# A convolution–attention block: output weights fetched with x on two DMA queues, zero fills earlier and partly on VectorE, PReLU as the larger of two linear forms, norms behind the match convolution

## The chip, the cores and the metric

The kernel runs on one core of a Trainium2 chip. The metric is the device time of one execution in microseconds (us); three timed runs before the change are shown, and one profiled execution of the same kernel.

## The reference, cut to what matters

Two images of 32 channels, 48 x 48, are normalised per channel. A cross-scale attention follows: a match image (1x1 convolution W1, 16 channels, full resolution), a reference image (W2, 16 channels, after 2x2 means) and an embedding (Wa, 32 channels). Each goes through a PReLU.

```
def prelu(x, a):
    return jnp.where(x >= 0, x, a * x)
embed_w  = prelu(conv1x1(x, Wa, ba), aa)
match_in = prelu(conv1x1(x, W1, b1), a1)
ref = prelu(conv1x1(x.mean over 2x2 blocks, W2, b2), a2)
w   = 3x3 patches of ref, each divided by its norm      # 576 keys
xp  = 3x3 patches of match_in                           # 2304 queries
yi  = softmax(10 * w . xp over the keys)
yt  = transposed convolution of yi with 6x6 patches of embed_w, stride 2
yd  = convolution of yt with Wd (3x3, stride 2) + bd, divided by 6
x   = x + yd
x   = x + DCT along h and w of the normalised x
```

## The kernel before

**Work in chunks.** The queries of an image are cut into six chunks of 8 rows x 48 columns (384 queries), each chunk into three tiles of 128 queries: 36 steps for both images. A step computes scores of one tile against 576 keys on TensorE (L707, four pairs of high and low fp32r parts), the row maximum on VectorE (L1156), the exponential on ScalarE (L899), the sum's reciprocal on VectorE (L1163) and the scaling on ScalarE (L907). GpSimd adds neighbouring rows of the softmax tiles (row sums, L528), TensorE turns the sums (L727, transposes by an identity, nine or eighteen to a group), ScalarE and VectorE split them (L915, L1171), and TensorE multiplies them by the embedded values (L742) and by the output weights (L754), which a chunk lags three chunks' steps behind. VectorE adds the result to x (L1194).

**The order.** Every engine has its own queue and runs it strictly in the order written. The list `BEFORE` holds what precedes the first step (image 0: statistics `xs`, `mean`, the split of x `low`, `weights`, `bias`, `conv2` in two parts, `conv1` in eight parts, `squares`, `norm`, `inorm`, `keys`, `split` of the first two chunks). `SPREAD` puts the jobs of image 1, and the embedding of image 0, into numbered gaps of the steps, three gaps to a step; each engine does its own share of a job when it comes to that gap. `split` of chunk g needs the im2col rows of chunk g in SBUF: ScalarE makes the high part, GpSimd the low part (L518, L522), and only then can TensorE compute that chunk's scores.

**A convolution part.** TensorE writes one of two PSUM banks (`pm`, L621 for `conv1` and `conv2`, L660 for the embedding; three matmuls for a `conv1` part). ScalarE writes the positive part `z` (L851), and in every second part the negative part `zneg` as well (L849); in the others VectorE makes it (L1072). VectorE then writes slope * zneg + z to the image (L1078). For the match image, rows that two overlapping blocks share are written a second time by further instructions of 48 columns (L1075, 14 for an image). A bank is free for the part after next when VectorE is done.

**DMA queues.** SyncE's queue issues, in this order: x of image 0 in four pieces (L363), the reference patches of image 0 (six transfers), the match patches of image 0 (36 transfers, L373 and L377), x for the residual (L411), x of image 1, the nine blocks of the output weights `wdf` (L405), the cosine matrix, x of image 1 for the residual, and then the patches of image 1. The small parameters `par` come on ScalarE's queue.

**GpSimd.** It fills the zeros (`zeros()`, L460 to L467) between `mean` and `squares`, and calls `output_weights()` after everything of `BEFORE`, ahead of its first row sum. That function begins with a wait for the nine `wdf` transfers.

```
            first = before.index(("low", 0, 0))
            perform(before[:first], handlers)
            zeros()
            pool.wait_ge(s_tiles, NTILE_EDGES)
            perform(before[first:], handlers)
            output_weights()
            for s in range(steps):
```

## Time and profile before

| | us |
|---|---|
| median of 3 timed runs | 326.76 (324.23 to 326.82) |
| profiled execution, whole | 326.36 |
| its span on the core | 324.6 |
| TensorE matmuls busy in the span | 259.4 |
| TensorE weight loads busy (beside the matmuls) | 240.2 |
| VectorE busy | 173.8 |
| ScalarE busy | 133.1 |
| GpSimd busy | 98.6 |

The profiled execution's own time stands 1.8 us above its span, for what lies around it. Busy shares are means over stages that have different limits, so the stretches have to be read one by one. The granted clock is given as a fraction of TensorE's full speed: 1.00 is 2.4 GHz and 0.50 is 1.2 GHz.

### The profile page before, as it was taken

How to read it: one execution, taken by the hardware profiler on the slowest of the kernel's cores; microseconds unless marked ns; L12 is line 12 of the kernel's file. 1: busy time of each engine (PE TensorE's matmuls, PEld its weight loads, DVE VectorE, ACT ScalarE, POOL GpSimd, SP SyncE). 2: the span in 40 equal slices, each digit the busy share in tenths (PEclk: the TensorE clock that was granted, in tenths of full speed). 3: DMA queues.
4: the chain of work that ended last, by engine and by line, in shares of the span. 5: the costliest groups of instructions: out<-in, count | busy, mean ns of one | idle time of the engine just before them, and what ended most of it. 6: DMA issues, size and time to landing. Idle time of an engine off the chain costs nothing.

```text
span 324.6 us, 4740 instructions
## 1 busy us (share of the span) xinstructions
PE 259.4 (80%) x1698; PEld 240.2 (74%) x1698; DVE 173.8 (54%) x368; ACT 133.1 (41%) x269; POOL 98.6 (30%) x101
## 2 busy tenths in 40 slices
PE   0459529936396979997998999999998899998075
PEld 0448428926375859996998989999987799997074
DVE  3864623254746673377225745555696854543822
ACT  2060236254346452445335674547645442122020
POOL 2710122038546220523514051517845600000000
PEclk9999999577657575599759999999999999999655
DMA  3030034420003000134300000000120000000241
GB/s 73 0 48 3 9 67 72 104 70 2 1 0 50 2 1 0 14 61 72 56 3 0 2 0 3 0 2 0 38 37 2 0 3 0 2 0 2 44 65 36
DMA packets 11495, 7.67 MB, mean 24 GB/s; under 512 B 8497, under 2 KB 10609, under 8 KB 11345
## 3 DMA queue, kind: packets, MB, share of 16 engines
q1 hardware_dynamic: 11264, 7.09, 12.2%
q10 hardware_dynamic: 208, 0.30, 0.3%
q8 instruction: 13, 0.21, 0.3%
q14 instruction: 10, 0.07, 0.1%
HBM read 2.14 MB, written 1.18 MB: 10 GB/s over the span
## 4 chain that ended last, share of the span: by engine, by line
PE 51%; DVE 20%; issue 9%; SPq 9%; ACT 6%; POOL 2%; DMA 2%; DVEq 0%; ACTq 0%; POOLq 0%
PE zt L727 20%; PE yt L742 8%; PE ps L707 5%; PE pm L681 4%; SPq L377 3%; SPq L373 3%; PE pm L621 3%; DVE negm L1156 3%; PE pm L774 3%; PE pm L660 2%; DVE mimg L1078 2%; DVE yl L1171 2%; DVE bnst L988 2%; PE pd L754 2%; DVE mimg L1075 2%
## 5 line engine op out<-in xcount | busy, mean ns | idle before, releaser
L727 PE MATMUL zt<-ident,nt 128*125 128x128 f32 (+1 forms) x720 | 98.0, 290 | 0.0
L727 PEld LDWEIGHTS zt<-ident,nt 128*125 128x125 f32 (+1 forms) x720 | 94.0, 191 | 1.4 <-issue 0.3
L528 POOL TENSOR_TENSOR nt<-nt 128x599 f32<-128x599 f32 (+1 forms) x42 | 56.4, 1342 | 47.9 <-ACT nt L907 40.8
L1171 DVE TENSOR_TENSOR yl<-zt,yh 125x384 fp32r<-125x384 f32 (+1 forms) x60 | 33.4, 557 | 43.9 <-ACT yh L915 15.2
L915 ACT ACTIVATE yh<-zt 125x384 fp32r<-125x384 f32 (+1 forms) x60 | 29.2, 486 | 44.1 <-PE zt L727 44.1
L899 ACT ACTIVATE nt<-ps,negm 128x576 f32<-128x576 f32 x32 | 23.7, 742 | 56.5 <-DVE negm L1156 56.5
L707 PE MATMUL ps<-wh,mh 128*128 128x288 f32 x64 | 18.3, 372 | 17.0 <-POOL mr L522 12.3
L907 ACT ACTIVATE nt<-nt,rps 128x599 f32<-128x599 f32 x36 | 28.6, 795 | 7.1 <-DVE rps L1163 6.9
L1156 DVE TENSOR_REDUCE negm<-ps 128x1 f32<-128x576 f32 x32 | 24.1, 753 | 13.1 <-PE ps L707 13.0
L742 PE MATMUL yt<-yh,kh 125*128 125x384 f32 (+1 forms) x60 | 25.6, 427 | 4.6 <-DVE yl L1171 4.5
L1194 DVE SCALAR_TENSOR_TENSOR v<-pd,v 32x384 f32<-32x384 f32 (+3 forms) x48 | 26.3, 547 | 2.4 <-PE pd L754 0.9
L518 POOL TENSOR_TENSOR ml<-vim,mh 128x384 fp32r<-128x384 f32 x12 | 12.1, 1005 | 49.4 <-ACT mh L871 49.2
L707 PEld LDWEIGHTS ps<-wh,mh 128*128 128x128 f32 x64 | 11.6, 222 | 19.5 <-POOL mr L522 12.7
L742 PE MATMUL yt<-yh,kl 125*128 125x384 f32 (+1 forms) x60 | 21.5, 359 | 0.0
L742 PE MATMUL yt<-yl,kh 125*128 125x384 f32 (+1 forms) x60 | 21.3, 356 | 0.0
L851 ACT ACTIVATE z<-pm,bias 96x288 f32<-96x288 f32 (+1 forms) x24 | 11.7, 491 | 16.2 <-PE pm L621 12.1
L484 POOL TENSOR_TENSOR mv<-mv,mhalf 32x1 f32<-32x1 f32 x2 | 1.1, 544 | 56.4 <-DVE mv L993 56.4
L742 PEld LDWEIGHTS yt<-yh,kh 125*128 125x128 f32 (+1 forms) x60 | 12.1, 201 | 7.5 <-DVE yl L1171 6.7
L621 PE MATMUL pm<-x4h,wsh 32*96 32x288 f32 x16 | 7.8, 496 | 10.3 <-DVE mimg L1078 9.1
L1163 DVE RECIPROCAL rps<-psm 128x1 f32<-128x1 f32 x36 | 5.9, 164 | 18.5 <-ACT nt L899 18.2
L707 PE MATMUL ps<-wl,mh 128*128 128x288 f32 x64 | 15.3, 324 | 0.0
L707 PE MATMUL ps<-wh,ml 128*128 128x288 f32 x64 | 15.2, 322 | 0.0
(165 smaller groups left out, 462.1 us busy)
## 6 DMA issues: line engine op xcount, KB each, us to landing
vim<-mimg SPq DMA_DIRECT2D x24, 72.0 KB, 2.5
v<-mimg SPq DMA_DIRECT2D x36, 24.0 KB, 1.9
x<-x SPq DMA_DIRECT2D x8, 72.0 KB, 2.9
vim<-mimg SPq DMA_DIRECT2D x12, 48.0 KB, 2.2
v<-x SPq DMA_DIRECT2D x2, 288.0 KB, 3.6
x_copy<-v SPq DMA_DIRECT2D x2, 288.0 KB, 2.9
xr<-x_copy SPq DMA_DIRECT2D x4, 144.0 KB, 3.1
out<-res SPq DMA_DIRECT2D x8, 72.0 KB, 2.4
```

The lines of the kernel that those rows point to most:

```text
L528: pool.tensor_tensor(nt[:, dst, (to + 1) * KP + 1:(to + 1) * KP + 1 + n], nt[:, one, (row1 + 1) * KP + 1:(row1 + 1) * KP + 1 + n], nt[:, o ...
L621: last = nc.tensor.matmul(o, w[rows, at:at + width], v, start=n == 0, stop=n == 2)
L681: last = nc.tensor.matmul(o[0:96, n:n + 1], sq[:, at:at + 96], ones[0:96, 0:1], start=r == 0, stop=r == 2)
L707: last = nc.tensor.matmul(scores_of(t)[:, i, 0:HALF], m[:, k, cols], w[b][:, HALF * i:HALF * (i + 1)], start=n == 0, stop=n == 3)
L727: last = nc.tensor.matmul(turned(zt[:, m % 2, :], n, dh, col, JW), keys_at(tile, r + dr, n, shift), ident[:, :], start=at == 0, stop=at == ...
L742: last = nc.tensor.matmul(yt[:, 0:CHUNK], e[b][0:n, blk, :], y[0:n, blk, :], start=blk == 0 and at == 0, stop=blk == KB - 1 and at == 2)
L899: nc.scalar.activation(strided(nt[:, tile_of(g, jb), :], KP + 1, (KP * HL // 2, 2), (KP, HL // 2), (1, WL)), strided(scores_of(t)[:, 0, :] ...
L907: nc.scalar.activation(tile, tile, ACT.Copy, scale=rps[:, k:k + 1]).then_inc(s_pn, 1)
L915: nc.scalar.activation(yh[0:n, blk, :].rearrange("p (h j) -> p h j", j=W), turned(zt[:, m % 2, :], n), ACT.Copy).then_inc(s_yh, 1)
L1156: nc.vector.tensor_reduce(negm[:, t % 2:t % 2 + 1], scores_of(t)[:, :, 0:HALF], AX.XY, ALU.max, negate=True).then_inc(s_mx, 1)
L1171: nc.vector.tensor_tensor(yl[0:n, blk, :].rearrange("p (h j) -> p h j", j=W), turned(zt[:, m % 2, :], n), F(yh[0:n, blk, :]).rearrange("p ...
L1194: nc.vector.scalar_tensor_tensor(out=image, in0=tap, scalar=1.0 / 6.0, in1=image, op0=ALU.mult, op1=ALU.add).then_inc(s_fin, 1)
```

## The change

1. **Loads.** Two of the four pieces of image 0's x go out on ScalarE's queue, ahead of `par`; SyncE issues the other two, then the nine `wdf` blocks, image 1's x, both residual copies of x and the cosine matrix, all ahead of the first patches.
2. **Zeros.** GpSimd does its zero fills first of all (`wdf` and the edges of `nt`). The fills of `emb`, `mr` and `wr` go to VectorE, at the end of `constants()`, ahead of the statistics. `output_weights()` on GpSimd stands ahead of `squares`.
3. **PReLU.** ScalarE writes slope * (y + bias) to `slanted`, and VectorE writes the larger of (y + bias) and `slanted` straight from PSUM: one instruction on each engine for every part. Where a slope is above 1 the larger form is the wrong one, so weights and biases are multiplied by a sign taken from the slope (`slope_signs()`, which waits for `par`), and the sign is undone in `kscale` and `wdf`. The doubled rows of the match image are no longer written part by part; two copies of 336 columns follow the last part.
4. **Order.** `bias` becomes three jobs, one for each convolution. The split of the big x (`low`) goes behind `conv2`; `norm` goes behind all eight parts of `conv1`. The weights of W2 come first on VectorE, then W1, then Wa. For image 1 the jobs `weights`, `bias`, `low`, `squares`, `norm`, `inorm` and `keys` sit in other gaps.

```
 BEFORE = [
-    ("xs", (0,)), ("mean", (0,)), ("low", (0,)), ("weights", (0,)), ("bias", (0,)), ("conv2", (0, 1)),
-    ("conv1", (0, 1)), ("squares", (0,)), ("conv1", (2, 3, 4)), ("norm", (0,)), ("conv1", (5, 6, 7)),
-    ("inorm", (0, 1)), ("keys", (0,)), ("split", (0, 1))]
+    ("xs", (0,)), ("mean", (0,)), ("weights", (0,)), ("bias", (0, 1)), ("conv2", (0, 1)), ("low", (0,)),
+    ("conv1", (0, 1)), ("squares", (0,)), ("conv1", (2, 3, 4, 5, 6, 7)), ("norm", (0,)),
+    ("inorm", (0, 1)), ("keys", (0,)), ("split", (0, 1)), ("bias", (2,))]
...
-    ("emb", 0, 2, 4, 2), ("ek", 0, 2, 9, 2), ("xs", 1, 1, 13, 1), ("mean", 1, 1, 15, 1), ("low", 1, 1, 17, 1),
-    ("weights", 1, 1, 20, 1), ("bias", 1, 1, 23, 1), ("residual", 0, 1, 28, 1), ("conv2", 1, 2, 26, 1),
-    ("conv1", 1, 8, 29, 1), ("squares", 1, 1, 33, 1), ("norm", 1, 1, 35, 1), ("inorm", 1, 2, 38, 1),
-    ("keys", 1, 1, 41, 1), ("emb", 1, 2, 46, 2), ("ek", 1, 2, 51, 2), ("residual", 1, 1, 60, 1),
+    ("emb", 0, 2, 4, 2), ("ek", 0, 2, 9, 2), ("xs", 1, 1, 13, 1), ("mean", 1, 1, 15, 1), ("weights", 1, 1, 19, 1),
+    ("bias", 1, 3, 22, 1), ("residual", 0, 1, 28, 1), ("conv2", 1, 2, 26, 1), ("low", 1, 1, 27, 1),
+    ("conv1", 1, 8, 29, 1), ("squares", 1, 1, 31, 1), ("norm", 1, 1, 37, 1), ("inorm", 1, 2, 40, 1),
+    ("keys", 1, 1, 42, 1), ("emb", 1, 2, 46, 2), ("ek", 1, 2, 51, 2), ("residual", 1, 1, 60, 1),
...
-            load_x(0)
+            load_x(0, range(2))
+            output_weights()
+            load_x(1, range(4))
+            for b in range(B):
+                sp.dma_start(x1(b), x[b].rearrange("c h w -> c (h w)")).then_inc(s_xin[b], 16)
+            sp.dma_start(cosm[:, :], dct).then_inc(s_cos, 16)
             ref_patches(0)
             match_patches(0)
-            sp.dma_start(x1(0), x[0].rearrange("c h w -> c (h w)")).then_inc(s_xin[0], 16)
-            load_x(1)
-            output_weights()
-            sp.dma_start(cosm[:, :], dct).then_inc(s_cos, 16)
-            sp.dma_start(x1(1), x[1].rearrange("c h w -> c (h w)")).then_inc(s_xin[1], 16)
...
             def output_weights():
 
                 pool.wait_ge(s_wdin, 1 + 16 * 9)
+                pool.wait_ge(s_sign, 1)
+                link(pool.tensor_tensor(wdf[:, :], wdf[:, :], sign[:, 2:3].to_broadcast([128, 128]), ALU.mult))
...
-            first = before.index(("low", 0, 0))
+            first = before.index(("squares", 0, 0))
+            zeros()
+            pool.wait_ge(s_tiles, NPOOL_EDGES)
             perform(before[:first], handlers)
-            zeros()
-            pool.wait_ge(s_tiles, NTILE_EDGES)
+            output_weights()
+            pool.wait_ge(s_wd, 1)
             perform(before[first:], handlers)
-            output_weights()
...
-                if k % 2:
-                    nc.scalar.activation(zneg[0:rows, 1, :], o[0:rows, 0:HALF], ACT.Relu,
-                                         bias=nbias[0:rows, which:which + 1], scale=-1.0)
-                nc.scalar.activation(z[0:rows, k % 2, :], o[0:rows, 0:HALF], ACT.Relu,
-                                     bias=bias[0:rows, which:which + 1]).then_inc(s_z, 1)
+                nc.scalar.activation(slanted[0:rows, k % 2, :], o[0:rows, 0:HALF], ACT.Identity,
+                                     bias=sbias[0:rows, which:which + 1],
+                                     scale=par[0:rows, P_A1 + which:P_A1 + which + 1]).then_inc(s_slant, 1)
...
+                nc.vector.memset(emb[:, :], 0.0).then_inc(s_zero, 1)
+                nc.vector.memset(F(mr[:, :, :]), 0.0).then_inc(s_zero, 1)
+                for b in range(B):
+                    nc.vector.memset(F(wr[b][:, :]), 0.0).then_inc(s_zero, 1)
+                dve.wait_ge(s_zero, 4)
...
+            def slope_signs():
+
+                dve.wait_ge(s_par, 48)
+                link(nc.vector.tensor_scalar(sign[:, :], par[:, P_A1:P_A1 + 3], 1.0, -2.0, ALU.is_gt, ALU.mult))
+                nc.vector.tensor_scalar_add(sign[:, :], sign[:, :], 1.0).then_inc(s_sign, 1)
+                dve.wait_ge(s_sign, 1)
+                link(nc.vector.scalar_tensor_tensor(out=kscale[:, :], in0=sign[:, 0:1], scalar=SOFTMAX_SCALE,
+                                                    in1=sign[:, 1:2], op0=ALU.mult, op1=ALU.mult))
...
+                dve.wait_ge(s_slant, k + 1)
+                w = list(dst.shape)[-1]
+                nc.vector.scalar_tensor_tensor(out=dst, in0=o[0:rows, 0:HALF].rearrange("p (h w) -> p h w", w=w),
+                                               scalar=bias[0:rows, which:which + 1],
+                                               in1=slanted[0:rows, k % 2, :].rearrange("p (h w) -> p h w", w=w),
+                                               op0=ALU.add, op1=ALU.max).then_inc(s_free["dve"], 1)
...
+                    nc.vector.tensor_copy(mimg[:, 1 + W:1 + CHUNK],
+                                          mimg[:, 1 + CHUNK * NCH:1 + CHUNK * NCH + n]).then_inc(s_dup[b], 1)
+                    nc.vector.tensor_copy(mimg[:, 1 + last:1 + last + n],
+                                          mimg[:, 1 + CHUNK + W:1 + 2 * CHUNK]).then_inc(s_dup[b], 1)
```

## Rows read from the trace of the kernel before

**Rows 1.** Stretches: start:end, length, busy (instructions) of PE, PEld, DVE, ACT, POOL; clock; DMA

```profile
0.00:46.40 46.40, 21.14 (x98) 17.88 (x98) 25.88 (x71) 12.61 (x24) 13.08 (x27) 1.00 0.18 33
46.40:70.90 24.50, 20.31 (x101) 18.71 (x101) 7.51 (x16) 12.09 (x25) 2.76 (x5) 0.77 0.41 79
70.90:96.40 25.50, 15.39 (x67) 13.62 (x67) 14.30 (x34) 10.26 (x22) 15.63 (x16) 0.63 0.02 7
96.40:123.00 26.60, 21.46 (x94) 18.15 (x93) 17.84 (x36) 15.19 (x30) 9.82 (x8) 0.63 0.10 16
123.00:145.00 22.00, 22.00 (x127) 21.39 (x128) 9.64 (x25) 8.02 (x18) 7.01 (x6) 0.66 0.14 25
145.00:170.00 25.00, 22.98 (x131) 21.26 (x130) 11.48 (x22) 9.37 (x21) 8.75 (x8) 0.80 0.26 45
170.00:299.00 129.00, 123.93 (x997) 119.04 (x995) 76.46 (x147) 62.31 (x128) 41.04 (x35) 1.00 0.03 6
```

**Rows 2.** Timeline up to the first reference convolution: start, length, engine and line, idle before

```profile
2.28 0.24 DVE L1029 MEMSET wsf<- 128x224 f32 x1
...
5.58 0.96 DVE L998 BATCH_NORM_STATS2 bnst<-x 128x6 f32<-128x288 f32 x2 [2.34 <-DMA x<-x]
...
8.45 0.68 POOL L484 TENSOR_TENSOR gm<-gm,mhalf 128x1 f32<-128x1 f32 x1 [1.67 <-DVE gm L1011]
...
9.59 1.04 DVE L1035 TENSOR_SCALAR nslope<-par 128x3 f32<-128x3 f32 x1
...
14.99 0.41 PE L621 MATMUL pm<-x2h,wsh 32*96 32x144 f32 x1
```

**Rows 3.** DMA issues by line: count, KB each, median us from issue to landing

```profile
par<-params ACTq DMA_DIRECT2D x1, 0.6 KB, 3.6
```

**Rows 4.** Timeline from the first convolution to the first scores

```profile
16.57 0.50 ACT L851 ACTIVATE z<-pm,bias 96x288 f32<-96x288 f32 x1 [9.43 <-PE pm L621]
...
18.41 0.52 PE L621 MATMUL pm<-x4h,wsh 32*96 32x288 f32 x1 [1.02 <-DVE wimg L1078]
...
26.17 5.89 PE L681 MATMUL pm<-ones,sq 96*96 96x1 f32 x36 [0.22 <-DVE mimg L1078]
...
37.00 2.85 PE L690 MATMUL pm<-ident,nrm 96*128 96x96 f32 x12 [0.76 <-DVE mimg L1078]
...
38.63 1.86 SPq L373 DMA_DIRECT2D vim<-mimg  x3
...
46.45 0.85 PE L707 MATMUL ps<-wh,mh 128*128 128x288 f32 x2 [6.61 <-POOL mr L522]
```

**Rows 5.** Instructions of lines 1078, 1072 and 1171: count, duration ns min/median/max, first and last start

```profile
L1078 DVE SCALAR_TENSOR_TENSOR mimg<-zneg,par,z x8: 515/516/1741, 20.9 to 124.4; 96x288 f32<-96x288 f32 x8
...
L1072 DVE TENSOR_SCALAR zneg<-pm,bias x12: 503/513/518, 17.2 to 156.5; 96x288 f32<-96x288 f32 x10, 128x288 f32<-128x288 f32 x2
...
L1171 DVE TENSOR_TENSOR yl<-zt,yh x60: 537/558/560, 100.4 to 298.4; 125x384 fp32r<-125x384 f32 x48, 100x384 fp32r<-100x384 f32 x12
```

**Rows 6.** Timeline, TensorE's two longest waits after the first scores

```profile
72.97 0.85 PE L707 MATMUL ps<-wh,mh 128*128 128x288 f32 x2 [5.67 <-POOL mr L522]
...
85.98 0.39 PEld L602 LDWEIGHTS pm<-gm,wsf 32*96 32x96 f32 x2 [6.04 <-DVE wsf L1044]
```

**Rows 7.** Chain of waits, 60 to 130 us: start, length, what

```profile
68.36 1.59 DMA wdf<-params
...
82.94 1.30 DVE wsh L1040
...
107.87 1.92 PE zt L727 x9
```

**Rows 8.** Chain of waits over the whole span, a piece of the late stage

```profile
195.17 1.97 PE zt L727 x18
```

**Rows 9.** Chain of waits, 96.4 to 123 us, pieces of the convolution parts on VectorE

```profile
102.79 0.53 DVE zneg L1072
...
103.80 1.75 DVE mimg L1078
```

More of the change, by code:

```diff
@@ L124, in program @@
     misc_no = {job: n for n, job in enumerate(plan)}
-    convs = parts_of(("conv2", "conv1", "emb"), plan)
+    convs = [job for job in plan if job[0] in ("conv2", "conv1", "emb")]
     def emptied(n):
@@ L359, in _, with load_x @@
         def _(sp):
-            def load_x(b):
+            def load_x(b, quarters):
                 src = x[b].rearrange("c h w -> c (h w)")
-                for r in range(4):
+                for r in quarters:
                     sp.dma_start(x4[b][C * r:C * (r + 1), :],
@@ new lines, in weights @@
+                one = slice(S_W1, S_W1 + 96)
+                nc.vector.tensor_scalar(wsf[:, one], par[:, P_W1:P_W1 + 96], root, sign[:, 0:1],
+                                        ALU.mult, ALU.mult).then_inc(s_scaled[b], 1)
+                dve.wait_ge(s_scaled[b], 2)
+                link(nc.vector.tensor_copy(wsh[:, one], wsf[:, one]))
+                nc.vector.tensor_tensor(wsl[:, one], wsf[:, one], F(wsh[:, one]), ALU.subtract).then_inc(s_wst[b], 1)
+                at = S_WA + 3 * C
@@ new lines, in weights, with biases @@
+                wa = slice(at, at + C)
+                nc.vector.tensor_scalar(wsf[:, wa], par[:, P_WA:P_WA + C], root, sign[:, 2:3],
+                                        ALU.mult, ALU.mult).then_inc(s_scaled[b], 1)
+                dve.wait_ge(s_scaled[b], 3)
+                link(nc.vector.tensor_copy(wsh[:, wa], wsf[:, wa]))
+                nc.vector.tensor_tensor(wsl[:, wa], wsf[:, wa], F(wsh[:, wa]), ALU.subtract).then_inc(s_wst[b], 1)
+            def biases(b, i):
+                o = group(dve, "bias", b, i)
+                rows, col = ((96, 1), (96, 0), (128, 2))[i]
+                link(nc.vector.scalar_tensor_tensor(out=bias[0:rows, col:col + 1], in0=par[0:rows, P_B1 + col:P_B1 + col + 1],
+                                                    scalar=sign[0:rows, col:col + 1], in1=o[0:rows, 0:1], op0=ALU.mult,
+                                                    op1=ALU.subtract))
+                nc.vector.tensor_tensor(sbias[0:rows, col:col + 1], bias[0:rows, col:col + 1],
+                                        par[0:rows, P_A1 + col:P_A1 + col + 1], ALU.mult).then_inc(s_free["dve"], 1)
@@ L1094, in ref_image @@
                 if i == 1:
+                    wait_emptied(dve, "conv2", b, 1)
                     edges(wimg[:, WL:], WL, HL, s_wimg[b])
             def match_image(b, i):
-                if b and i == 0:
-                    for t in range(NCH):
-                        dve.wait_ge(s_mim[t], 16 * IM2COL * b)
                 if i == 0:
                     dve.wait_ge(s_const, 4)
-                at = 1 + W * i
-                first, last = (W * ROWS * (BLOCKS - 1) - W, 0), (W, (NCH - 1) * W)
-                above = [first] * (i > 0)
-                below = [last] * (i < ROWS - 1)
-                more = [(mimg[:, at + to:at + to + W], lambda v, n=n: v[:, n:n + W]) for to, n in above + below]
-                prelu("conv1", b, i, 96, 0, strided(mimg[:, :], CHUNK + at, (CHUNK, NCH), (1, W)), *more)
-                if i == ROWS - 1:
+                    if b:
+                        for t in range(NCH):
+                            dve.wait_ge(s_mim[t], 16 * IM2COL * b)
+                at = CHUNK + 1 + W * i
+                prelu("conv1", b, i, 96, 0, strided(mimg[:, :], at, (CHUNK, NCH), (1, W)))
+                if i == ROWS - 1:
+                    wait_emptied(dve, "conv1", b, i)
+                    n, last = CHUNK - W, CHUNK * (BLOCKS - 1)
+                    nc.vector.tensor_copy(mimg[:, 1 + W:1 + CHUNK],
+                                          mimg[:, 1 + CHUNK * NCH:1 + CHUNK * NCH + n]).then_inc(s_dup[b], 1)
+                    nc.vector.tensor_copy(mimg[:, 1 + last:1 + last + n],
+                                          mimg[:, 1 + CHUNK + W:1 + 2 * CHUNK]).then_inc(s_dup[b], 1)
+                    dve.wait_ge(s_dup[b], 2)
                     edges(mimg, W, ROWS * BLOCKS, s_mimg[b])
@@ L1245, in _ @@
             constants()
-            perform(before, handlers)
+            slope_signs()
+            perform(before[:before.index(("squares", 0, 0))], handlers)
+            nc.vector.tensor_scalar_mul(bd6[64:128, :], par[64:128, P_BD:P_BD + 1], 1.0 / 6.0).then_inc(s_bd6, 1)
+            perform(before[before.index(("squares", 0, 0)):], handlers)
             maximum(0)
```

132 lines of the change are left out of this document (52 added, 80 removed).

## The prediction

> **What bounds the kernel now.** I read the stretches first, then the timeline up to the first scores, then the chain of waits where TensorE stands idle. The stretches [rows 1] show stages with different limits. Up to 46.4 us TensorE is busy 21.1 of 46.4 us: a serial chain through all engines. From 46.4 to 123 us it is busy 57.2 of 76.6 us: waits in between. From 170 to 299 us it is busy 123.9 of 129 us at a granted clock of 1.00 (2.4 GHz): there TensorE is the bound, so whatever is gained earlier moves this stage to the left whole. The tail behind 299 us isn't touched.
>
> The longest waits behind the first scores are two [rows 6]. At 72.97 TensorE had waited 5.67 us for the low part of chunk 2 on GpSimd. The reader should look at what stands ahead of that on GpSimd: the output weights, whose last transfer lands at 69.95 [rows 7], because SyncE issues the 36 match patches first (from 38.63, three in 1.86 us [rows 4]). At 85.98 TensorE had waited 5.8 to 6.0 us for the scaled weights of image 1 on VectorE [rows 6]. From 96.4 to 123 us the chain runs through VectorE's pieces of the match convolution again and again [rows 9].
>
> **The change part by part.** The sum is made against the profiled execution, 326.36 us (span 324.6); it stands 0.4 us below the median of the runs, so I add 0.3 at the end.
>
> (a) *Up to the first scores.* Loss: VectorE gets four more fills, 600 + 768 + 2 x 576 = 2520 columns; a fill of 224 took 0.24 us [rows 2], so 2.7 us. From the end of its constants at 2.1 us they and the three old fills (1.1 us) end at 5.9. Then `slope_signs` waits for `par`. It now goes out behind two pieces of x, some 0.9 us later: last issue about 2.55, and 3.6 us to land [rows 3] makes 6.15. Three small linked instructions add 0.7 us, so the statistics begin at 6.9 in place of 5.58 [rows 2]: +1.3 us. That x lands earlier is worth nothing, since `par` and the fills come last. Gain: today 5.86 us pass from the root (9.13) to the first reference matmul (14.99) [rows 2]. In these VectorE splits x, and its small instructions run beside GpSimd's fills (1.04 us for three columns, 9.59 [rows 2]). After the change four instructions of about 0.3 us and two small matmuls stand there, about 1.6 us. Root at 10.45, first reference matmul at 12.05: -2.9 us. The split of x is moved behind `conv2` in VectorE's queue (0.75 us), and `conv1` waits for it. `conv2` takes TensorE 2.45 us, then one instruction on ScalarE (0.50 [rows 4]) and one of 0.52 on VectorE, the edges and the split: `conv1` starts at 16.8 in place of 18.41 [rows 4], -1.6.
>
> A part of `conv1` then costs 1.05 us on TensorE, 0.50 on ScalarE and 0.52 on VectorE with about 0.2 of semaphores; with two banks that is 2.25 us for two parts, against 3.4 now. The two squares on ScalarE (1.4 us) cost about 0.6 once. Eight parts end at 26.9; the two copies (0.3 each) and edges lead to the first match patch at 28.0, against 38.63 [rows 4]. This gain of 10.6 us isn't on the path. What is late next is the keys: norms 25.8 to 31.7 (5.89 us [rows 4], the same matmuls), then VectorE and GpSimd 1.7 us, then 2.85 us of matmuls, from 33.4 and no longer from 37.00 [rows 4]: -3.6. What follows (scaling, two casts on ScalarE, the high and the low part of the first query chunk) took until 46.45; it loses the 1.4 us in which it waited for patches, which are long there now. First scores at 41.4: **-5.0 us**, between -3 (the new VectorE form costs twice what I take) and -6.
>
> (b) *The output weights.* They are issued between 1.6 and 6.5 us and land before 9; GpSimd waits for them ahead of `squares`, when its queue is empty. Queued behind that wait on GpSimd are the squares, which can't start before 16 anyway; its pooled sums and power of image 0 stand ahead of it. So the 5.67 us stall goes. The price of the move on SyncE: sixteen more transfers stand ahead of the reference patches and two fewer, at 0.5 to 0.6 us each; they end near 10 us, 6 us before the patches are ready, so they cost nothing. Next late would be ScalarE's exponential (ready at 66.9 in today's times, where TensorE ended at 67.3). **-5.7 us**, low end -3, if GpSimd's saved-up row sums come between.
>
> (c) *Second stall, up to the first turn at 96.4.* ScalarE also stood idle here for GpSimd's pooled x of image 1, which came late behind the same wait; that x is loaded at 10 us now. I rebuild the chain: two scores of 2.05 us each at the half clock, the exponential and reciprocal, nine weight instructions (some 5 us today, ending just ahead of 86.9 us, with 1.30 us for a cast of 96 columns [rows 7]; without anything beside them 0.3 each, 2.6 us; I take 4, as GpSimd is still about half busy), maximum, exponential, maximum, exponential, scores. From scores 6 to the first turn this makes 17 us, against 23.4. The bias matmuls need just their own weights now, so TensorE waits little. **-6.5 us**, between -3 and -9.
>
> The Trainium skill (SBUF — State Buffer, section Who interferes with whom) says that a copy on VectorE can take a port that GpSimd shares, and that the second to come is held until the first has finished. By that rule the two new copies of image 1 can each stand behind a row sum of 1.3 us. The trace agrees in kind, with the cast of 1.30 us.
>
> (d) *Match convolution of image 1, 96.4 to 123.* Today a part costs VectorE 1.1 to 1.6 us undisturbed and up to 2.7 when a GpSimd addition runs beside it: the combining instruction took 516 ns in the median and 1741 at most, while those that read PSUM never passed 518 or, with one operand in SBUF, 560 over 60 instances [rows 5]. The new one reads PSUM and one SBUF operand, so I take 0.52 to 0.56 for it. One part's pieces run from 102.79 to 105.55 in the chain [rows 9], 2.7 us; five such groups lie on it, about 10.7 us in all, of which 2.6 would stay. But TensorE was busy 21.46 of 26.6 us [rows 1], so at the same clock it is the next bound after 5.1 us. **-4 us**, between -2 and -5.
>
> (e) *TensorE's clock.* Nine turns took 1.92 us at 0.50 [rows 7], eighteen took 1.97 at 1.00 [rows 8]. The stretches between 70.9 and 145 ran at 0.63 to 0.66 [rows 1], and after both stalls the trace shows 0.50 again. With the stalls gone some of the 59 us of busy TensorE there may run at the full clock; the embedding, during which the clock fell each time, stays. I take **-2 us**. If half of the missing third came back it would be -10; if the fuller chain met a worse pattern, +4.
>
> The Trainium skill (TensorE: Matmul & The Clock Gate, Part 4: PE-mode transpose) says that the full clock doesn't engage for transposes. By it this term would be nil for the turns. The trace doesn't agree: the late stage is mostly turns, at 1.00.
>
> Sum: -5.0 - 5.7 - 6.5 - 4.0 - 2.0 = -23.2; 326.36 - 23.2 = 303.2, with the 0.3 from above **303.5 us**.
>
> **The rivals.**
> - *The queues of GpSimd and VectorE are late next.* Once the wait is gone, three row sums, the pooled x, a power and two query splits come close together; then (b) gives 3 and (c) 3, (d) 2, (e) nothing: 326.4 - 13 = 313. For it: GpSimd was busy 15.6 of 25.5 us up to 96.4 [rows 1]. Against: part of that was saved-up work.
> - *The clock comes back.* -10 in (e) and -5 in (d): 294. For it: 123 to 145 us has no idle TensorE at all and still 0.66 [rows 1], so there is room. Against: nothing in the change makes a matmul larger.
> - *The weights still come late*, so that (b) stays: 309. Against: the issue needs just GpSimd's first fill.
> - *Slower: the late stage loses its full clock.* It holds 123.9 us of matmuls at 1.00 [rows 1]. Each microsecond of it at 0.50 costs one more (1.92 against 0.98 for nine turns). From 21 us of such work on, the gain of (a) to (d) is gone; with a quarter of the stage, 31 us, the time is 326.4 - 21 + 31 = 336. It would need stalls, and the change doesn't touch that stage.
>
> **How the numbers follow.** Forecast 0.62 (298 to 309), late queues 0.15, clock back 0.17, weights late 0.02, slower 0.02, and 0.02 for a gain and loss that cancel. The range 291 to 314 takes in the first two rivals and the bounds of (a), (c) and (e). Three runs spread by 0.8%, so about 1% is what a measurement can tell from no change. Faster by over 1%: 0.96; within: 0.02; slower: 0.02.
>
> **What would show it.** First scores near 41.4; the first match patch issued near 28; no wait of GpSimd for `wdf` after 20 us; chunk 2's scores about 10.7 us earlier than 72.97; the first turn near 79; the maximum instruction at 0.52 to 0.56 us for both images; clock above 0.65 between the first turn and the late stage. The prediction is wrong if the statistics start later than 7.5 us, if VectorE's wait for weights stays above 4 us, or if the clock term is several times its size either way.

## The result and the profile after

The changed kernel takes 312.07 us in the median of four runs (309.75 to 316.12), the kernel before 326.16 in the same series; the ratio is 0.955, with a 95% interval of 0.946 to 0.964. The profiled execution takes 313.37 us, 13.0 less than that of before (326.36). Forecast were 303.5 us, range 291 to 314. The direction is right and the time lies at the slow end of the range: of the 23.2 us in the sum, 13 to 14 are there. Executions of one kernel differ by up to 2% with TensorE's granted clock (309.75 us at a mean of 0.878, 316.12 at 0.847 here), so runs over 1.5% above the fastest of their kernel are left out of all ratios and intervals, while the medians and ranges in us are of all runs.

The best view for a chain of steps is the start of each step's exponential on ScalarE (read from its timeline, one per step):

| step | before | after | shift | shift since the line above |
|---|---|---|---|---|
| 0 | 49.57 | 48.10 | -1.5 | |
| 5 | 70.30 | 68.15 | -2.2 | -0.7 |
| 6 | 77.92 | 71.23 | -6.7 | -4.5 |
| 8 | 87.61 | 80.78 | -6.8 | -0.1 |
| 10 | 96.69 | 90.26 | -6.4 | +0.4 |
| 13 | 132.61 | 113.06 | -19.6 | -13.1 |
| 14 | 140.88 | 122.88 | -18.0 | +1.6 |
| 17 | 160.24 | 147.77 | -12.5 | +5.5 |
| 18 | 171.67 | 158.08 | -13.6 | -1.1 |
| 35 | 251.75 | 238.24 | -13.5 | +0.1 |

From step 18 on the schedule is rigid: seventeen steps shift by 0.1 us in all. That part of the prediction held: everything is decided before 170 us. Two disappointments stand in the table, the first 1.5 us and the nothing between steps 6 and 10, and one surprise, the 13 us between steps 10 and 13, of which 6 come back later.

The timeline of the changed kernel up to the first scores (start, length, engine and line, idle before) answers to [rows 2] and [rows 4]:

```profile
1.91 3.16 DVE L1035 TENSOR_SCALAR comb<-comb 128x128 f32<-128x128 f32 x1
...
6.88 0.95 DVE L1003 BATCH_NORM_STATS2 bnst<-x 128x6 f32<-128x288 f32 x2
...
9.75 0.69 POOL L480 TENSOR_TENSOR gm<-gm,mhalf 128x1 f32<-128x1 f32 x1 [3.44 <-DVE gm L1016]
...
13.81 0.40 PE L622 MATMUL pm<-x2h,wsh 32*96 32x144 f32 x1 [1.12 <-DVE sbias L1083]
...
17.81 0.76 DVE L1029 TENSOR_TENSOR x4l<-x,x4h 128x576 fp32r<-128x576 f32 x1
...
18.67 0.52 PE L622 MATMUL pm<-x4h,wsh 32*96 32x288 f32 x1 [2.48 <-DVE x4l L1029]
...
28.42 5.89 PE L684 MATMUL pm<-ones,sq 96*96 96x1 f32 x36 [0.67 <-DVE mimg L1097]
...
30.12 1.86 SPq L373 DMA_DIRECT2D vim<-mimg  x3
...
36.04 2.88 PE L693 MATMUL pm<-ident,nrm 96*128 96x96 f32 x12 [1.73 <-POOL nrm L507]
...
45.02 0.82 PE L710 MATMUL ps<-wh,mh 128*128 128x288 f32 x2 [4.24 <-DVE wr L1170]
```

The last of the small parameters on ScalarE's queue, issued at 2.61 us (line, KB, median us from issue to landing):

```profile
par<-params ACTq DMA_DIRECT2D x1, 0.6 KB, 2.7
```

Statistics and root are where they were forecast (6.9 and 10.45). Then TensorE waits 1.12 us for `sbias` and 2.48 us for `x4l`. Both are VectorE instructions that nothing but their place in the queue makes late. The first line is a case of its own: an instruction that took 0.23 us now takes 3.16, while GpSimd's fills run from 1.97 to 4.99 us. It lies on the chain to the statistics: `par` has landed at 5.3 us, VectorE's last fill ends at 6.24 and `slope_signs` starts right behind it, at 6.28. From the lengths of VectorE's fills, 2.3 us for the four new and 1.0 for the three old, I estimate that they would have ended near 5.6, so the slow instruction costs about 0.6 us.

Around the second stall, answering to [rows 6] and [rows 7] (same columns):

```profile
70.45 0.75 DVE L1174 TENSOR_REDUCE negm<-ps 128x1 f32<-128x576 f32 x1
70.58 0.59 PE L593 MATMUL pm<-mv,comb 128*128 128x2 f32 x2 [3.57 <-DVE mv L1007]
...
75.96 2.58 POOL L526 TENSOR_TENSOR nt<-nt 128x599 f32<-128x599 f32 x2
75.98 1.29 DVE L1060 CAST wsh<-wsf 128x96 fp32r<-128x96 f32 x1
...
77.31 1.34 DVE L1061 TENSOR_TENSOR wsl<-wsf,wsh 128x96 fp32r<-128x96 f32 x1
...
80.00 0.75 DVE L1174 TENSOR_REDUCE negm<-ps 128x1 f32<-128x576 f32 x1
```

Read the GpSimd line against the two VectorE lines behind it: two row sums of 1.29 us, and beside each of them one weight instruction of 1.29 to 1.34 us. The step's maximum (80.00) stands behind all nine. It is the same 5.0 us block as before the change. Earlier, at 70.58, TensorE has waited 3.57 us for image 1's statistics, and the scores of step 7 stand behind that.

The PReLU's two instructions are in the page's list of costliest groups (count, busy, mean ns, idle before):

```profile
L850 ACT ACTIVATE slanted<-pm,sbias,par 96x288 f32<-96x288 f32 (+1 forms) x24 | 13.9, 586 | 26.6 <-PE pm L622 14.1
...
L1097 DVE SCALAR_TENSOR_TENSOR mimg<-pm,bias,slanted 96x288 f32<-96x288 f32 x16 | 8.2, 514 | 17.0 <-ACT slanted L850 12.8
```

VectorE's is as taken, 0.51 us in image 1 as well as in image 0. ScalarE's is 0.59, not 0.50.

The stretches between the same steps (10 to 14, then 14 to 18) in both kernels; columns as in [rows 1]. The kernel before:

```profile
96.70:140.90 44.20, 39.06 (x186) 35.15 (x186) 24.61 (x53) 19.88 (x40) 15.35 (x13) 0.61 0.10 16
140.90:171.70 30.80, 28.78 (x176) 27.01 (x175) 15.35 (x30) 13.03 (x28) 11.56 (x9) 0.83 0.26 45
```

The changed kernel, and its late stage in a stretch of its own:

```profile
90.30:122.90 32.60, 31.78 (x179) 28.50 (x179) 14.88 (x35) 18.55 (x35) 15.44 (x13) 0.71 0.16 25
122.90:158.10 35.20, 31.56 (x186) 29.96 (x186) 16.06 (x31) 12.96 (x27) 10.72 (x9) 0.80 0.21 36
...
160.00:286.00 126.00, 120.92 (x971) 116.07 (x969) 74.73 (x145) 60.78 (x124) 39.31 (x33) 1.00 0.03 6
```

Steps 10 to 14 take 11.6 us less. TensorE's idle time falls from 5.1 to 0.8 us, 4.3 of them; the other 7.3 are busy time, with the granted clock at 0.71 in place of 0.61. Busy time multiplied by the clock is 23.8 and 22.6, so a small part of the 7.3 is work that now stands behind step 14. Steps 14 to 18 give 4.4 us back, 1.6 as idle time (one wait of 3.53 us at 136.43 for VectorE's split of a turn, in place of two waits of 1.1 and 0.8) and 2.8 as busy time. Over both stretches the work is the same, 47.7 and 47.8 us at the full clock. Of the 7.2 us that steps 10 to 18 gain, 2.7 are idle time and 4.5 are the higher clock.

### The profile page after: what moved, and what is told of

Same layout as the page of the kernel before. It is cut to its first block, busy times and chain, and to the rows that moved or that the text cites. A ratio compares the mean times of both kernels' runs of the same rounds, so it can differ in the third digit from the quotient of the medians.

```text
span 311.6 us, 4697 instructions
## 1 busy us (share of the span) xinstructions
PE 255.3 (82%) x1698; PEld 237.3 (76%) x1698; DVE 160.0 (51%) x343; ACT 130.9 (42%) x257; POOL 96.8 (31%) x98
## 3 DMA queue, kind: packets, MB, share of 16 engines
HBM read 2.14 MB, written 1.18 MB: 11 GB/s over the span
## 4 chain that ended last, share of the span: by engine, by line
PE 62%; DVE 21%; issue 8%; ACT 7%; POOL 1%; DVEq 0%; ACTq 0%; POOLq 0%
PE zt L730 21%; PE ps L710 8%; PE yt L745 8%; PE pm L662 6%; PE pm L622 4%; DVE negm L1174 3%; PE pm L684 3%; PE pm L777 3%; DVE yl L1189 3%; PE pd L757 2%; DVE bnst L993 2%; ACT nt L899 2%; DVE v L1212 2%; PE zt L710 2%; PE pm L693 2%
## 5 line engine op out<-in xcount | busy, mean ns | idle before, releaser
L730 PE MATMUL zt<-ident,nt 128*125 128x128 f32 (+1 forms) x720 | 94.8, 284 | 0.0
L730 PEld LDWEIGHTS zt<-ident,nt 128*125 128x125 f32 (+1 forms) x720 | 90.8, 186 | 1.1 <-issue 0.2
L899 ACT ACTIVATE nt<-ps,negm 128x576 f32<-128x576 f32 x32 | 23.8, 745 | 47.5 <-DVE negm L1174 47.5
L745 PE MATMUL yt<-yh,kh 125*128 125x384 f32 (+1 forms) x60 | 24.7, 411 | 7.1 <-DVE yl L1189 7.0
L850 ACT ACTIVATE slanted<-pm,sbias,par 96x288 f32<-96x288 f32 (+1 forms) x24 | 13.9, 586 | 26.6 <-PE pm L622 14.1
L745 PE MATMUL yt<-yh,kl 125*128 125x384 f32 (+1 forms) x60 | 20.6, 344 | 0.0
L745 PE MATMUL yt<-yl,kh 125*128 125x384 f32 (+1 forms) x60 | 20.6, 343 | 0.0
L710 PEld LDWEIGHTS ps<-wh,mh 128*128 128x128 f32 x64 | 11.6, 222 | 10.0 <-issue 5.2
L1097 DVE SCALAR_TENSOR_TENSOR mimg<-pm,bias,slanted 96x288 f32<-96x288 f32 x16 | 8.2, 514 | 17.0 <-ACT slanted L850 12.8
L710 PE MATMUL ps<-wr,mr 128*128 128x288 f32 x64 | 15.6, 331 | 0.0
```

Source lines behind the costliest of these rows:

```text
L710: last = nc.tensor.matmul(scores_of(t)[:, i, 0:HALF], m[:, k, cols], w[b][:, HALF * i:HALF * (i + 1)], start=n == 0, stop=n == 3)
L730: last = nc.tensor.matmul(turned(zt[:, m % 2, :], n, dh, col, JW), keys_at(tile, r + dr, n, shift), ident[:, :], start=at == 0, stop=at == ...
L745: last = nc.tensor.matmul(yt[:, 0:CHUNK], e[b][0:n, blk, :], y[0:n, blk, :], start=blk == 0 and at == 0, stop=blk == KB - 1 and at == 2)
L850: nc.scalar.activation(slanted[0:rows, k % 2, :], o[0:rows, 0:HALF], ACT.Identity, bias=sbias[0:rows, which:which + 1], scale=par[0:rows, ...
L899: nc.scalar.activation(strided(nt[:, tile_of(g, jb), :], KP + 1, (KP * HL // 2, 2), (KP, HL // 2), (1, WL)), strided(scores_of(t)[:, 0, :] ...
```

## The experiments

The experiments ran in three series, each with the kernel before beside it: 325.74 us for the load order alone, the old PReLU with the new load order and the two single edits; 325.65 for the old load order with the new PReLU, the norm in the middle, the old gaps and both edits; 325.24 for the rest. Medians are of 6 or 12 runs of the kernel. Ratios are to the kernel before, with 95% intervals. Between series compare ratios. The changed kernel was profiled twice, at 313.37 and 315.14 us; the second execution is 1.8 us later from step 3 on, and where that matters both are given.

### The load order alone

On the kernel before: the output weights and image 1's x ahead of the patches on SyncE, GpSimd's wait ahead of the squares.

```
             load_x(0)
+            output_weights()
+            load_x(1)
+            for b in range(B): sp.dma_start(x1(b), ...)
+            sp.dma_start(cosm[:, :], dct).then_inc(s_cos, 16)
             ref_patches(0)
             match_patches(0)
...
             zeros()
             pool.wait_ge(s_tiles, NTILE_EDGES)
+            output_weights()
+            pool.wait_ge(s_wd, 1)
             perform(before[first:], handlers)
-            output_weights()
```

> The kernel before with one part of the change: the output weights, image 1's x and the residual copies issued ahead of the patches, and GpSimd's output_weights ahead of the squares. Theory (the wait for wdf on GpSimd held chunk 2): the scores of step 6 move from 72.97 us to about 67.4, all later steps with them, and the time is 320 to 321 against 326. Rival (GpSimd's saved-up row sums and image 1's statistics are late next and hand most of it back by the first turn): first turn earlier by 2 us or less, time 323 to 325.

Measured: 322.91 us, ratio 0.992 (0.987 to 0.996). From the exponential of step 5 to that of step 6 it takes 3.1 us in place of 7.6, so the stall is gone as computed. But step 5 itself had come 2.1 us later in the profiled execution, 1.2 of them at step 3, beside the embedding, and of 3.6 us ahead at step 16 1.0 was left at step 18. The gain in the medians, 2.8 us, is half of the stall, nearer to the rival (323 to 325) than to the theory (320 to 321).

### The changed kernel with the old PReLU

```
-                nc.scalar.activation(slanted[...], o[0:rows, 0:HALF], ACT.Identity, bias=sbias[...], scale=par[...])
+                if k % 2:
+                    nc.scalar.activation(zneg[0:rows, 1, :], o[0:rows, 0:HALF], ACT.Relu, bias=nbias[...], scale=-1.0)
+                nc.scalar.activation(z[0:rows, k % 2, :], o[0:rows, 0:HALF], ACT.Relu, bias=bias[...])
...
 (VectorE: the old three to five instructions for a part, doubled rows part by part, no block copies)
```

> The changed kernel with the old PReLU (positive and negative parts, rows of the match image doubled part by part), everything else as changed. Theory (the PReLU form is the largest part of the gain, through VectorE): first scores about 4 us later, exponential of step 13 about 8 us later, time 320 to 324 against 312. Rival (the gain behind step 10 came from the order of the norms and from TensorE's clock, not from the PReLU): 313 to 316.

Measured: 326.63 us, ratio 0.999 (0.994 to 1.005), slower than either theory. Without the new PReLU nothing is left of the gain. First exponential at 52.08 us, 4.0 later than in the changed kernel and 2.5 later than before the change; step 13 14.9 us later than in the changed kernel (13.0 by its second execution).

### The changed kernel with the old load order, and both old

```
             load_x(0, range(2))
-            output_weights() ... (and the x copies)
             ref_patches(0)
             match_patches(0)
+            sp.dma_start(x1(0), ...); load_x(1, range(4)); output_weights(); ...
...
-            output_weights()
-            pool.wait_ge(s_wd, 1)
             perform(before[first:], handlers)
+            output_weights()
```

> The changed kernel with the old place of the output weights (issued behind the 36 match patches, GpSimd waiting for them ahead of its first row sum) and of image 1's x. Theory (the load order is worth what the stall was, 5 us, and the rest of the change doesn't depend on it): scores of step 6 about 5 us later than in the changed kernel, time 316 to 318. Rival (the load order alone gave 2.8 us in the median, because VectorE and TensorE's clock took the rest; with faster image 1 parts behind it the clock is kept or lost in other places): 313 to 315, or over 319 if both parts need each other.

> The changed kernel with both the old PReLU and the old load order; what stays is the new order of the jobs, the zero fills and the three bias jobs. It closes the square of the two parts. Theory (they overlap: the PReLU form starts the match patches some 6 us earlier, so that the output weights behind them on SyncE's queue land in time even in their old place; without the new PReLU the load order counts in full): about 329 to 331, that is 3 to 5 us over the old PReLU with the new load order (326.6), where with the new PReLU the load order was worth 1 to 2. Rival (the load order is worth the same 1 to 2 us in both): 327.5 to 328.5.

Measured: 313.21 us (0.965, 0.960 to 0.970) with the new PReLU and 326.86 us (0.995, 0.990 to 1.001) with the old one, against 312 and 326.6 with the new load order. The load order is worth 0.4 to 1.1 us in the medians of the first pair (1.5 to 3.1 by the ratios), which the intervals don't separate from none, and nothing in the second. My theory of the overlap was right for one corner and wrong for the other. The timeline with the old load order and the new PReLU shows why no stall came back (SyncE's issues, then GpSimd's first instruction behind the wait):

```profile
55.81 4.13 SPq L405 DMA_DIRECT2D wdf<-params  x9
...
61.47 0.40 POOL L501 TENSOR_TENSOR wdf<-wdf,sign 128x128 f32<-128x128 f32 x1 [15.29 <-issue]
```

SyncE issues the weights from 55.81 us and no longer from 64.64, because the match patches ahead of them start at 29.5 in place of 38.63; GpSimd is through by 62.8 us and then waits for chunk 2's high part on ScalarE, which comes at 64.3. With the old PReLU the patches start at 32.9, still 5.7 earlier than before, since `norm` no longer cuts the convolution in two, and GpSimd starts at 64.2, 5.0 us ahead of the low part of chunk 2 (69.2). So the rest of the change keeps the stall away by itself. That it does so through the place of `norm` is argued, not shown: putting `norm` back moves the patches by 6 us (below), but this kernel also comes to step 5 3.4 us later than the kernel before (73.67 for 70.30), which gives the weights more time.

### Two waits in the start of the changed kernel

The weights as three jobs, each bias of image 0 ahead of the next weights, and the split of x ahead of `conv2`.

```
-    ("xs", (0,)), ("mean", (0,)), ("weights", (0,)), ("bias", (0, 1)), ("conv2", (0, 1)), ("low", (0,)),
+    ("xs", (0,)), ("mean", (0,)), ("weights", (0,)), ("bias", (0,)), ("weights", (1,)), ("bias", (1,)),
+    ("weights", (2,)), ("low", (0,)), ("conv2", (0, 1)),
```

> The changed kernel, with image 0's weights as three jobs, each bias worked out ahead of the next weights, and the split of the big x ahead of conv2. Theory (conv2 waited 1.12 us for a PSUM bank that VectorE emptied only behind all nine weight instructions, and conv1 2.48 us for the split behind conv2): conv2 starts at 13.1 in place of 13.81, conv1 at 16 to 16.5 in place of 18.67, first scores at 42.6 in place of 45.0, time 309.5 to 310. Rival (what follows the convolution, the norms on GpSimd and ScalarE's casts, is late anyway): first scores move by less than 1 us, 311.5 to 312.5.

Measured: 308.47 us, ratio 0.953 (0.947 to 0.958); first exponential at 45.27, 2.8 us ahead of the changed kernel, still 2.4 ahead at step 18. Its timeline:

```profile
12.85 0.41 PE L623 MATMUL pm<-x2h,wsh 32*96 32x144 f32 x1
...
13.99 0.75 DVE L1030 TENSOR_TENSOR x4l<-x,x4h 128x576 fp32r<-128x576 f32 x1
...
15.78 0.52 PE L623 MATMUL pm<-x4h,wsh 32*96 32x288 f32 x1 [0.53 <-DVE wimg L1105]
```

No wait for `sbias` any more, and the match convolution starts 2.9 us earlier (15.78 for 18.67) with the same instructions.

### GpSimd's row sums wait for image 1's weights

```
             for s in range(steps):
+                if s == 6:
+                    pool.wait_ge(s_wst[1], 2)
```

> The changed kernel, but GpSimd's row sums from step 6 on wait until VectorE has split image 1's weights. Theory (the nine weight instructions take 5.0 us at 75.1 to 80.1 us because casts of 96 columns are held by row sums of 1.3 us beside them): they take 2.6 us, the exponential of step 8 comes 2.4 us earlier, time 309.5 to 310.5. Rival (they are slow for another reason, or the later row sums delay the first turn as much): unchanged within 0.5 us, 312 or 313.

Measured: 310.47 us, ratio 0.955 (0.950 to 0.961). Its timeline:

```profile
76.78 1.04 DVE L1059 TENSOR_SCALAR wsf<-par,gm,sign 128x96 f32<-128x96 f32 x1
...
77.86 0.21 DVE L1062 CAST wsh<-wsf 128x96 fp32r<-128x96 f32 x1
...
78.10 0.26 DVE L1063 TENSOR_TENSOR wsl<-wsf,wsh 128x96 fp32r<-128x96 f32 x1
...
79.71 0.75 DVE L1176 TENSOR_REDUCE negm<-ps 128x1 f32<-128x576 f32 x1
```

The same cast takes 0.21 us and the same difference 0.26, five to six times less than beside a row sum; only the first one, beside the query split (76.76 to 77.75), takes 1.04. The exponential of step 8 follows that of step 7 by 4.63 us in place of 6.65. That is 2.0 of the 2.4 us expected; the nine instructions take 3.0 us in place of 5.0. In the time the edit alone doesn't show (312.07 to 310.47, both ratios 0.955). On top of the first edit it does: 0.953 (0.947 to 0.958) becomes 0.940 (0.935 to 0.946), in the next table.

### Both edits, and the norm back in the middle

```
-    ("squares", (0,)), ("conv1", (2, 3, 4, 5, 6, 7)), ("norm", (0,)),
+    ("squares", (0,)), ("conv1", (2, 3, 4)), ("norm", (0,)), ("conv1", (5, 6, 7)),
```

> Both small edits together: biases ahead of the next weights, the split ahead of conv2, and the row sums waiting for image 1's weights. Theory (they act in stretches that follow one another in a serial chain, and the schedule behind step 18 is rigid): first scores 2.8 us and step 8 another 2 us earlier than in the changed kernel, time 306 to 307. Rival (TensorE's clock takes one of them back): 308 to 309, as with the first alone.

> The changed kernel with image 0's norm back between the fifth and the sixth part of the match convolution. Theory (the match patches have 7 us to spare before ScalarE casts them, the keys are last, and the 5.9 us of norm matmuls stand in series ahead of them): the norms start at 24 to 25 in place of 28.4, the matmuls that spread them near 34.6 in place of 36.04, first scores 1 to 1.5 us earlier, time 310.5 to 311. Rival (the last three parts are delayed by 5.9 us and their end becomes what the keys wait for): no gain or up to 2 us later, 312 to 314.

> Biases and split early, the row sums waiting for image 1's weights, and image 0's norm back in the middle of the match convolution. Theory (the norm in the middle brought first scores 1.0 us earlier by itself, and with a convolution that starts 2 us earlier the spare time of the patches stays): first scores another 1 us earlier than with two edits (45.3 to 44.3), time 304 to 305. Rival (as in the median of the norm alone, TensorE's clock takes it back): 305 to 306.

> The changed kernel as it is, again, so that the others of this series have it beside them on the same chip. Expected by every theory: 0.955 of the time before, 311 to 312, with a spread of 1% between executions that goes with the granted clock.

| kernel | median us | ratio (95%) | first exponential | step 8 |
|---|---|---|---|---|
| changed, again | 312.80 | 0.960 (0.954 to 0.966) | 48.06 | 82.67 |
| norm in the middle | 312.31 | 0.962 (0.957 to 0.968) | 47.13 | 81.64 |
| two edits | 305.31 | 0.940 (0.935 to 0.946) | 45.29 | 77.72 |
| all three | 306.24 | 0.943 (0.938 to 0.947) | 44.32 | 76.66 |

The two edits add up. The kernel with all three edits stands in one series with the changed kernel, and the intervals don't meet: 306.24 by 312.80, 2% under it. The norm in the middle brings the first exponential 0.9 to 1.0 us earlier both times, the low end of what was expected, and shows in neither median. Its timeline:

```profile
24.60 5.92 PE L685 MATMUL pm<-ones,sq 96*96 96x1 f32 x36
...
33.73 3.03 PE L694 MATMUL pm<-ident,nrm 96*128 96x96 f32 x12
...
36.17 1.87 SPq L374 DMA_DIRECT2D vim<-mimg  x3
...
41.24 0.52 ACT L872 ACTIVATE mh<-vim 128x384 fp32r<-128x384 f32 x1 [1.79 <-DMA v<-mimg]
```

The patches pay for it: they start 6 us later than in the changed kernel, and that is more than they had to spare. ScalarE waits 1.79 us for them, the scores wait for the low part of the first queries and no longer for the keys, and of 2.3 us gained at the matmuls that spread the norms (33.73 for 36.04) 1.0 is left at the scores.

### Image 1's norm, inorm and keys in their old gaps

```
-    ... ("squares", 1, 1, 31, 1), ("norm", 1, 1, 37, 1), ("inorm", 1, 2, 40, 1), ("keys", 1, 1, 42, 1)
+    ... ("squares", 1, 1, 33, 1), ("norm", 1, 1, 35, 1), ("inorm", 1, 2, 38, 1), ("keys", 1, 1, 41, 1)
```

> The changed kernel with image 1's squares, norm, inorm and keys in the gaps where they stood before. Theory (of the 13 us that were gained between steps 10 and 13 only what VectorE's chain gave stays, the rest is the 5.9 us norm standing ahead of step 13 or behind it): step 13 about 5 us later, step 18 within 1 us of the changed kernel, time 311 to 313. Rival (the place behind the convolution is worth the norm's time): step 18 and the time 3 to 6 us later, 315 to 318.

Measured: 315.36 us, ratio 0.966 (0.958 to 0.973), runs from 311.17 to 317.72. Step 13 is 10.5 us later than in the changed kernel, step 17 2.1 and step 18 4.8; by its second execution, which agrees with this one at step 3, 8.6, 0.2 and 3.0. So the better part of the 13 us peak in the first table is order (the norm ahead of step 13 or behind it). The theory of less than 1 us at step 18 falls. In the medians the new gaps are 2.6 to 3.3 us better, but the intervals overlap, and whether anything of that is real stays open.

### Filler matmuls in TensorE's waits

On the kernel with two edits, twelve matmuls of 128 x 128 into the bank of the output taps, ahead of its first use.

```
+            def filler(n):
+                for _ in range(n):
+                    nc.tensor.matmul(pd[:, 0:128], ident[:, :], ident[:, :], start=True, stop=True)
...
+                if s == 8: filler(4)
                 if s + 1 < NT: scores(s + 1)
+                if s == 5: filler(5)
+                if s == 7: filler(3)
```

> The kernel with two edits (305.3) and twelve extra matmuls of 128 x 128 into a bank that nobody reads yet, in TensorE's three waits of 3.6, 1.8 and 2.3 us around steps 5 to 8. Theory (the 0.50 clock from about 76 to 92 us follows from these waits, and costs several us because TensorE is busy throughout there): the granted clock between 75 and 95 us rises to 0.8 or more, the exponentials of steps 9 to 11 come 3 to 6 us earlier, time 300 to 303. Rival (the clock there has another cause, such as the small bias matmuls and the convolution's 32-row operands, or is given back before step 18): clock still 0.5, 305 to 306.

Measured: 307.95 us, ratio 0.948 (0.942 to 0.953). Stretches with TensorE's busy time, clock and DMA, and the wait for image 1's statistics; first with the filler, then without:

```profile
69.78 0.38 PE L596 MATMUL pm<-mv,comb 128*128 128x2 f32 x2 [2.46 <-DVE mv L1020]
...
76.00:92.00 16.00, 14.48 (x65) 0.58 0.07 9
...
104.00:125.00 21.00, 20.26 (x142) 0.84 0.23 39
```

```profile
69.72 0.38 PE L596 MATMUL pm<-mv,comb 128*128 128x2 f32 x2 [3.59 <-DVE mv L1010]
...
76.00:92.00 16.00, 13.54 (x57) 0.51 0.07 9
...
104.00:125.00 21.00, 20.25 (x166) 1.00 0.23 38
```

What the theory forecast didn't come: the clock from 76 to 92 us rose by 0.07, steps 9 to 11 moved by less than 0.1 us, and further on the clock was lower. But the fillers closed only part of the waits: from 3.59, 1.50 and 2.34 us they fell to 2.46, 0.50 and 1.40. So this shows that waits about 1 us shorter don't bring the clock back; what keeps it at 0.50 there stays open.

## Why the prediction was right in direction and off in size

**What bounds the kernel.** Right: a gain ahead of step 18 shifts all behind it, to 0.1 us.

**(a) First scores: -5.0 forecast, -1.4 measured** (46.45 to 45.02), outside its own bounds. The statistics start at 6.88 and the root is ready at 10.45, as forecast, but that took some luck: `par` landed at 5.3 us, not 6.15 (2.7 us from issue, not 3.6), and VectorE's fills ended at 6.24, not 5.9, behind the instruction of 3.16 us that I had at 0.23. The step that failed is "four instructions of about 0.3 us and two small matmuls stand there, about 1.6 us": I looked at what `conv2` computes with and not at the PSUM bank it writes to. That bank is the one of the first bias, and VectorE empties it only behind the weights of all three convolutions; 3.4 us passed, not 1.6. The delay runs on through the split of x behind `conv2`, so `conv1` started at 18.67, not at 16.8. The experiment with early biases and early split recovered 2.8 us, which shows these two together. Two parts of `conv1` took 2.3 us, and 2.7 with the squares, not 2.25 (ScalarE 0.59 for 0.50): 0.75 us more up to the norms. The last 1.0 us lies behind the norms (8.98 us from 36.04 to the scores, 8.0 forecast): GpSimd splits the first queries now just beside VectorE's split of the keys, whose second instruction took 1.44 us in place of 0.75 and third 1.13 in place of 0.45, and the scores wait for the keys. With the norm in the middle, where GpSimd's split comes behind, the two take 0.75 and 0.45 again.

**(b) The stall on the output weights: -5.7 forecast; -4.5 measured at the exponential of step 6.** The wait is gone, and scores of step 6 come 7.2 us earlier (65.73). What I had not on the list of late ones is the maximum of step 6: it stands behind image 1's statistics on VectorE and starts at 70.45, though its scores end at 67.0. The cause I gave, the new load order, does remove it when made alone (3.1 us from step 5 to step 6 in place of 7.6), but the changed kernel doesn't need it: with the old order the stall stayed away as well, because the patches ahead of the weights start 9.1 us earlier there. Two parts of the change remove the same stall, and I would have counted it twice had I costed the earlier patches, which I called "isn't on the path". In the old load order they are on it: they stand ahead of the output weights.

**(c) Up to the first turn: -6.5 forecast, nothing measured** (-6.7 at step 6, -6.4 at step 10). This is the largest miss, and the step of the prediction that failed here is the rebuilt chain of 17 us from the scores of step 6 to the first turn: it took 25.1 (65.73 to 90.85), 23.4 before. It rested on nine weight instructions shrinking from 5.0 to 4 us and on scores that were held by saved-up work. The instructions took 5.0 us again. The experiment with the waiting row sums brought step 8 2.0 us nearer to step 7, so row sums beside them are the cause of that much. The chain had two more things wrong. The scores of step 7 don't follow those of step 6: TensorE waits 3.57 us for image 1's statistics in between. And from step 8 to step 10 it takes 9.5 us, 9.1 before; eight one-column matmuls of the last bias (1.86 us at 83.95) stand there now, and before they followed TensorE's wait for the weights (86.65). No experiment takes these two apart. I had seen the 1.30 us cast and named the mechanism, then took a value near the middle for no better reason than that GpSimd is busy half of the time. But the weights stand right behind the reciprocal of step 7, which also releases the scaling and with it the row sum; the row sum of step 6 was still queued ahead of it. So they met in both traces, before and after. The rule of the Trainium skill (SBUF — State Buffer, section Who interferes with whom), which I set against the two block copies, held here for the casts (1.29 us beside a row sum, 0.21 without); the first copy of image 1 took 0.64 us in place of 0.33, and that costs little.

**(d) and (e): -4 and -2 forecast, -7.2 measured from step 10 to step 18.** The sum is right, the split isn't. VectorE's chain was worth 4.3 us of TensorE's idle time in steps 10 to 14, as in (d), but 1.6 of them come back by step 18, which leaves 2.7 for the 4 forecast. The clock gave 4.5 in all, for 2. The square of the PReLU and the load order shows the same stage: between steps 10 and 14 with both old parts, and in the changed kernel run beside it (columns as in [rows 1]):

```profile
95.90:138.40 42.50, 39.59 (x179) 35.59 (x180) 25.50 (x51) 19.76 (x40) 15.52 (x13) 0.58 0.13 22
```

```profile
92.20:124.80 32.60, 31.75 (x179) 28.52 (x179) 14.91 (x35) 18.47 (x35) 15.42 (x13) 0.71 0.16 25
```

Of 9.9 us, 2.1 are idle time and 7.8 the same instructions at 0.71 in place of 0.58. The PReLU is worth 13.7 to 14.6 us in the medians (326.86 - 313.21 and 326.63 - 312.07) and 9.9 to 14.3 by the ratios, most or all of the gain; more than half of it works through TensorE's clock (7.8 of the 13.7 us between these two traces at step 18). By which property of TensorE's work the clock rises isn't shown, and the filler experiment doesn't settle it. The zero fills on VectorE were never undone by themselves, so their share is known from the timeline alone.

**The rivals.** "The queues of GpSimd and VectorE are late next", at 313 us and 0.15, came nearest, in time and in mechanism: what it gave (b), 3, and (c), 3, was measured as 4.5 and 0. That its 313 is so near 312.07 is luck: it took 5 for (a), where 1.4 came, and 2 for (d) and (e), where 7.2 came. I had spoken against it with "part of that was saved-up work". The clock rival was right for one stage and gave part of it back in the next. The rival that ends slower and the one with late weights didn't come.

**The signs.** The first match patch goes out at 30.12 (28 forecast) and the first turn at 90.85 (79), step 6's scores come 7.2 us earlier (10.7), VectorE's new instruction takes 0.51 to 0.52 us in both images, and the clock between the first turn and the late stage is 0.71 and 0.80, above 0.65. Of the three signs of being wrong one came true, if "VectorE's wait for weights" is read as its block of weights: 5.0 us, above 4.

**The transposes.** Nine turns took 0.98 to 1.18 us on the chain at the 1.00 clock, and the late stage (160 to 286 us), 71.6 of its 120.9 busy us turns, ran at 1.00 throughout. So for this kernel the trace keeps its disagreement with the rule of the Trainium skill (TensorE: Matmul & The Clock Gate, Part 4: PE-mode transpose).

## What to carry to other kernels

Before costing a step that is moved up, write down for each of its operands, its output bank among them, the last instruction in its engine's queue that must have run: here the bank of a finished one-column matmul was held by six unrelated instructions. When two parts of a change may remove the same wait, undo each in the changed kernel as well as adding it to the old one; alone, the load order was worth 2.8 us, on top of the rest nothing that could be told from none. Where an instruction is slow beside another engine's, ask if the same event releases both: then expect them to meet every time, and half is no estimate.

## What the runs showed of the hardware that was not expected

One kernel's executions differ by TensorE's clock pattern. Two profiled executions of the changed kernel agree within 0.12 us up to step 2 and are 1.8 us apart at step 3 (56.11 and 57.95): from 49 to 56 us, beside the embedding, the granted clock is 0.95 in the one and 0.84 in the other. So a profile's single step can't show an effect under 2 us in such a stage, and an edit's gain of 1 us (the norm in the middle) can be real in its place and invisible in the median.

The recorded clock can be wrong at the start. It reads 1.00 up to 46.4 us in [rows 1] and from 20 to 45 us in the changed kernel. But a matmul of 288 columns starts every 0.24 us there (19.00, 19.24 and 19.48 in the changed kernel), as at 0.50 later, and from 49.43 us on a pair of them takes 0.27 us. So up to about 49 us the matmuls went at the pace of the low level.

An instruction of VectorE of 128 x 128 from and to SBUF (0.23 us in the kernel before, where GpSimd's large fills stand later) took 3.16 us while GpSimd did nothing but fill zeros, and it was held through four fills in a row, not through one; VectorE's own fills, which overlap the last of GpSimd's, took 0.54 to 0.70 us for 576 to 768 columns, no more for a column than the 224 in 0.24 us.
